# First pass of a two-layer attention kernel: pair tiles between the image tiles, or all behind them

## What is computed

```python
# layer 0: pair_rep is the group-normed x
x = (pair_rep - mu) * rsqrt(var + EPS) * ln_w + ln_b
bias = einsum('hc,bcij->bhij', wb, x)            # 4 heads, added to the scores
scores = einsum('bhcij,bhcik->bhijk', q, k) * scale + bias[:, :, None, :, :]
...
# layer 1
bias = einsum('nijz,zh->nhij', pair_repr, bias_proj)[:, None]   # 8 heads
sim = softmax(einsum('nsqhc,nskhc->nshqk', q, k) * scale) + bias
```

## Time and profile before

| | |
|---|---|
| median of 3 runs | 4822.93 us (4820.17 to 4829.05) |
| the profiled execution | 4825.53 us, its span 4823.7 us |
| mean granted TensorE clock over the span | 0.975 |
| busy over the span | PE 95%, PE weight load 81%, DVE 81%, ACT 78%, POOL 75% |
| DMA | 383.12 MB, mean 79 GB/s over the span |
| first four of 40 slices (0 to 482 us) | 355, 351, 346, 198 GB/s |

### The profile page before, as it was taken

How to read it: one execution, slowest core, us unless ns; L and a number is a source line. 1 busy time by engine, 2 the same in 40 slices (tenths; PEclk the granted TensorE clock), 3 DMA queues, 4 the chain that set the end, 5 groups by cost and what they waited for, 6 DMA issues and landing times. The chain is left out here.

```text
span 4823.7 us, 153371 instructions
## 1 busy us (share of the span) xinstructions
PE 4606.1 (95%) x46135; PEld 3896.8 (81%) x46135; DVE 3924.8 (81%) x12976; ACT 3768.1 (78%) x11664; POOL 3626.7 (75%) x6054
## 2 busy tenths in 40 slices
PE   5667999999999999999999989999999999999998
PEld 1225888888888888888888868888888888888887
DVE  4444888889888988898888968888888888888887
ACT  2336888888888888888888868888888888888886
POOL 3443888888888888888888847777777777777776
PEclk8678999999999999999999989999999999999999
DMA  9996111111111111111111111111111111111111
GB/s 355 351 346 198 58 53 61 52 61 52 61 52 61 53 57 56 53 60 52 61 52 61 53 45 48 52 52 52 52 52 52 52 52 52 52 52 52 52 52 34
DMA packets 237387, 383.12 MB, mean 79 GB/s; under 512 B 18756, under 2 KB 156616, under 8 KB 224968
## 3 DMA queue, kind: packets, MB, share of 16 engines
q1 hardware_dynamic: 237256, 381.63, 23.3%
HBM read 309.21 MB, written 72.35 MB: 79 GB/s over the span
## 5 line engine op out<-in xcount | busy, mean ns | idle before, releaser
L1507 POOL TENSOR_SCALAR l_probs<-l_probs,l_inv 128x256 f32<-128x256 f32 x2048 | 941.5, 479 | 377.5 <-DVE l_inv L1404 377.5
L663 POOL TENSOR_SCALAR l_probs<-l_probs,l_inv 128x256 f32<-128x256 f32 x2048 | 947.8, 477 | 268.5 <-DVE l_inv L914 268.5
L832 ACT ACTIVATE l_probs<-l_probs,l_neg_max 128x256 f32<-128x256 f32 x2048 | 1021.0, 518 | 0.8 <-DVE l_neg_max L906 0.6
L1305 ACT ACTIVATE l_probs<-bank,l_neg_max 128x256 f32<-128x256 f32 x2048 | 942.5, 476 | 46.4 <-DVE l_neg_max L1398 39.4
L906 DVE CUSTOM_DVE_ANT_0 l_probs<-bank,bias 128x256 f32<-128x256 f32 x2048 | 779.9, 418 | 201.1 <-PE bank L773 197.1
L1411 DVE TENSOR_TENSOR l_probs_t<-bank,bias 128x512 f32<-128x512 f32 x1024 | 669.7, 685 | 131.0 <-PE bank L1217 116.0
L1398 DVE TENSOR_REDUCE l_neg_max<-bank 128x2 f32<-128x512 f32 x1024 | 675.0, 682 | 43.1 <-PE bank L1205 33.9
L773 PE MATMUL bank<-ident,l_probs 128*128 128x128 f32 x4096 | 629.5, 276 | 1.1 <-POOL l_probs L663 0.7
L1217 PE MATMUL bank<-ident,l_probs 128*128 128x128 f32 x4096 | 560.0, 274 | 5.3 <-POOL l_probs L1507 3.9
L786 PE MATMUL bank<-l_probs_t,l_v 128*64 128x256 f32 x4096 | 498.5, 385 | 0.2 <-issue 0.2
L773 PEld LDWEIGHTS bank<-ident,l_probs 128*128 128x128 f32 x4096 | 463.9, 141 | 36.8 <-POOL l_probs L663 1.7
(11 more groups left out here) (205 smaller groups left out, 14710.2 us busy)
## 6 DMA issues: line engine op xcount, KB each, us to landing
fp_x<-in_x_dram SPq DMA_DIRECT2D x32, 1024.0 KB, 6.4
fp_ln_w<-in_L_conv_ln_w_dram SPq DMA_DIRECT2D x32, 1024.0 KB, 8.5
fp_ln_b<-in_L_conv_ln_b_dram SPq DMA_DIRECT2D x32, 1024.0 KB, 11.1
fp_pair<-in_L_conv_pair_repr_dram SPq DMA_DIRECT2D x32, 1024.0 KB, 10.6
l_x<-in_x_dram SPq DMA_DIRECT2D x128, 256.0 KB, 2.9
l_ln_w<-in_L_conv_ln_w_dram SPq DMA_DIRECT2D x128, 256.0 KB, 3.3
l_ln_b<-in_L_conv_ln_b_dram SPq DMA_DIRECT2D x128, 256.0 KB, 3.5
x<-l_y SPq DMA_DIRECT2D x128, 256.0 KB, 2.0
```

What stands on the lines that cost most here:

```text
L663: last = nc.gpsimd.tensor_scalar(probs[:, h, c], probs[:, h, c], inv[:, h, c:c + 1], 1.0, ALU.mult, ALU.mult)
L832: last = nc.scalar.activation(probs[:, h, c], probs[:, h, c], ACT.Exp, bias=neg_max[:, h, c:c + 1], scale=-1.0, accum_out=total[:, h, c:c ...
L1305: last = nc.scalar.activation(probs[:, h, c], b_s[h % 4][:, c * W:(c + 1) * W], ACT.Exp, bias=neg_max[:, h, c:c + 1], accum_out=total[:, h ...
L1507: last = nc.gpsimd.tensor_scalar(probs[:, h, c], probs[:, h, c], inv[:, h, c:c + 1], 1.0, ALU.mult, ALU.mult)
```

## The change

All 32 image tiles are run first, and all 32 pair tiles behind them. `over_tiles` is left with image tiles only, in rounds of four with the first peeled. `late_pairs` becomes all tiles. SP loads the first four pair buffers in the last round, once image tile 31 has been issued, and no longer at the start. The statistics and the reload of the parts keep their places relative to the first pair tiles (third to sixth, and second). No operation, size or buffer differs.

```diff
-        def over_tiles(engine, image_tile, image_end, pair_tile):
-            def body(t, first, last):
-                for k in range(2 * PAIR_BUFS):
-                    image = 2 * PAIR_BUFS * t + k, PAIR_BUFS * t + k // 2, k % 2
-                    image_tile(*image)
-                    if last and k == 2 * PAIR_BUFS - 1:
-                        pair_tile(PAIR_BUFS * t + k // 2, t, k // 2)
-                        image_end(*image)
-                    else:
-                        image_end(*image)
-                        if k % 2:
-                            pair_tile(PAIR_BUFS * t + k // 2, t, k // 2)
-            loop_ends_peeled(engine, TILES // (2 * PAIR_BUFS), body)
-        late_pairs = range(TILES // 2, TILES)
+        def over_tiles(engine, image_tile):
+            def body(t):
+                for k in range(4):
+                    image_tile(4 * t + k, 2 * t + k // 2, k % 2)
+            loop_first_peeled(engine, TILES // 4, body)
+        late_pairs = range(TILES)
...
-            for i in range(PAIR_BUFS):
-                load_pair(i, i)
             def body(t, first, last):
-                for k in range(2 * PAIR_BUFS):
-                    if not (last and k >= 2 * PAIR_BUFS - 2):
-                        load_image(2 * PAIR_BUFS * t + k + 2, k % 2)
-                    if last and k == 2 * PAIR_BUFS - 1:
-                        load_pair(PAIR_BUFS * (t + 1) + k // 2, k // 2)
-                        store_pair(PAIR_BUFS * t + k // 2, k // 2)
-                        store_image(2 * PAIR_BUFS * t + k, k % 2)
-                    else:
-                        store_image(2 * PAIR_BUFS * t + k, k % 2)
-                        if k % 2:
-                            load_pair(PAIR_BUFS * (t + 1) + k // 2, k // 2)
-                            store_pair(PAIR_BUFS * t + k // 2, k // 2)
-            loop_ends_peeled(sp, TILES // (2 * PAIR_BUFS), body)
+                for k in range(4):
+                    if not (last and k >= 2):
+                        load_image(4 * t + k + 2, k % 2)
+                    elif k == 2:
+                        for i in range(PAIR_BUFS):
+                            load_pair(i, i)
+                    store_image(4 * t + k, k % 2)
+            loop_ends_peeled(sp, TILES // 4, body)
```

More of the change, by code:

```diff
@@ L423, in image_tile @@
                 project(b_part[B_PART], m.wb_t[:], bt[i]).then_inc(projected[B_PART], 1)
-            def image_end(tile, t, i):
                 pe.wait_ge(weighted, tile + 1)
@@ L441, in pair_project @@
                 project(b_pair, m.w_pair[:], turned[i % 2]).then_inc(pair_projected, 1)
[L443 to L447, removed]
+            over_tiles(pe, image_tile)
             pair_turns(late_pairs[0], late_pairs[0] // PAIR_BUFS, 0)
@@ L481, in pair_out @@
                 nc.scalar.activation(pair_evac[i][:], b_pair[:], ACT.Copy).then_inc(pair_evacuated, 1)
[L483 to L487, removed]
+            over_tiles(act, image_tile)
             pair_copies(late_pairs[0], late_pairs[0] // PAIR_BUFS, 0)
@@ L531, in image_tile @@
                 nc.gpsimd.tensor_tensor(wt[i][:], xt[i][:], wt[i][:], ALU.mult).then_inc(weighted, 1)
-            over_tiles(pool, image_tile, lambda tile, t, i: None, lambda tile, t, i: None)
+            over_tiles(pool, image_tile)
 def finish_statistics(nc, m, pieces):
```

## The result

The changed kernel takes **4838.29 us** (median of 9 runs, 4835.99 to 4839.75), the kernel before on the same chip 4824.85 us (9 runs): ratio 1.0028 [1.0017, 1.0038], slower by 13.4 us. The forecast was 4834.3 us (4822 to 4850), +11.4 us over the kernel before. The profiled execution took 4838.70 us, its span is 4836.9 us.

A forecast was written before the change was run, and what follows sets the result against it. The prediction took the serial PE, POOL, ACT order to bound the mixed image stretch and DMA the pair tiles alone. Terms -40.8 + 51.0 + 1.2 = +11.4 us on 4822.93 gave 4834.3 us, range 4822 to 4850.

The forecast's parts named there:

- Image stretch, step 9.45: Image tiles without pair tiles between them: 9.45 us a tile, 31 steps in 293.0 us against 333.75, a gain of 40.8.
- The buffer loop: Reuse of the two image buffers, from projection through reload to landing: 18.9 us for two tiles, 9.45 a tile.
- the ring: Serial chain in an image tile: PE projects, POOL multiplies, PE projects the product, ACT copies it out; 9.33 us a tile.
- D: Image tile loads, from the first load's issue to the landing of all three parts: forecast 10.04 us.
- C: Image tile, from the start of the weights' projection to the next load's issue into that buffer: forecast 8.76 us.
- The wait between landing and projection: Image tile, PE's wake after its loads have landed: forecast within 0.1 us.
- Rival 1, step 9.33: Image stretch: step at the ring's 9.33 us, cold start hidden, no measurable difference; +6.5 us, 4829.4; chance 0.19.
- Rival 2, faster by the clock: Image stretch: PE's clock rises and stays up, step 8.6 us; -16.2 us, 4806.7; chance 0.07.
- Rival 3, landings of 11.3 us: Image stretch: loads stay slow without pair tiles, step 10.1 us; +30.9 us, 4853.8; chance 0.12.
- The pair stage, +51.0: Pair tiles alone, DMA bound: sixteen more tiles at 3.19 us each add 51.0 us.
- the seam, +1.2: Passage from image to pair tiles: PE arrives cold, so first transposes take longer; +1.2 us, between 0 and 3.4.
- The moves that "cost nothing": Statistics chain, bias reload and DVE bias operations behind pair tiles, and SP's moved pair loads at 0.4 us an issue: 0.

The follow-up runs named there:

- early loads: Changed kernel, but each part of an image tile is loaded as soon as its own buffer is free: 4826.3 us, 1.0002 of the kernel before.
- second banks: Changed kernel, but even and odd image tiles project into PSUM banks of their own: 4840.9 us, 1.0033 of the kernel before.
- filler: Changed kernel plus 24 unused transposes per image tile keeping PE busy: 4838.1 us; with each part loaded once its buffer is free, 4817.9; also with separate banks, 4818.8.
- the four kernels whose loops had been opened: Changed kernel with early loads plus second banks (4814.5 us), plus filler (4817.9), plus both (4818.8), or plus both and stores issued by ScalarE (4815.5).

## Why the prediction was right, and where it was not

*Image stretch, step 9.45.* Measured 9.50, -39.3 us for -40.8. The buffer loop is the bound, as forecast, though narrowly: eight of the 31 steps are the ring's 9.34. Two terms are off and offset each other. D is 10.30 in the mean for 10.04, because the earlier trace rows give one good load, while eight of 30 took 10.6 us or more: +0.13 on the step. C is 8.52 for 8.76, because some product projections were warm: -0.12. The wait between landing and projection is 0.24 for 0.1. The prediction had left the warm projections out against the late loads, so the balance was foreseen, with no number for the loads. That the loop binds is shown by early loads (12 us) against second banks (none).

*Rival 1, step 9.33.* Wrong by the same small margin; with the other loop shortened the step did fall to 9.14.

*Rival 2, faster by the clock.* The clock stayed low (0.62), so its condition did not come about. The filler runs show that its price was wrong as well: it took D to be fixed. With the clock at 0.87 the step was 9.43 and not 8.6, because D grew by what C lost (0.99 and 0.94 us). The Trainium skill (TensorE: Matmul & The Clock Gate, "What's actually happening") has activity release the throttle; the trace agrees: 0.59 without and 0.87 with the filler, from 100 to 280 us.

*Rival 3, landings of 11.3 us.* Three of the first loads came to 11.2 or 11.3, the rest to 11.0 or less; the median is 10.06. Without pair tiles in the queue ln_b landed 9.1 us after its own issue in the median, against 11.1 in the earlier trace rows.

*The pair stage, +51.0, and the seam, +1.2.* Together 52.2 forecast, 51.4 measured. The tiles of the stage are 3.21 us apart for 3.19. Counted from the first pair load behind the reload (344.19, 382.29 before) the stage took 51.5 us more, so the seam's +1.2 is not there at the end: PE lost 0.9 us on the first 32 transposes, the next loads went out 1.1 us later, and by 344.19 us that had been absorbed. The moves that "cost nothing" leave no trace in this sum; PE's idle time behind the reload is 8.90 us (355.19), and 9.05 before. One of their sizes was wrong: SP took 11.32 us for the four pair loads in one go, not 4 x 0.4 (1.81 us with rows of 8 KB). The store of image tile 30 went out at 324.72, over 4 us after its last copy, and nothing waited for it.

*The start.* 1.3 us later, where the prediction had 0. The change is not needed to explain it: runs whose code there is the same began between 26.25 and 28.42 us.

*The layers.* -0.2 us; the prediction had none.

*The absolute time* is 4.0 us above the forecast: 2.0 from the sum, and 1.9 because the kernel before took 4824.85 us beside it and not 4822.93.

*The rate of HBM.* The prediction set aside the Trainium skill's 358 GB/s of the HBM side (DMA: Bandwidth & Descriptors, "Where 436 GB/s comes from") for the 2.5 us per MB of the earlier trace rows. For the changed kernel that was right: its D is made of such loads, and 341 GB/s is what the loop asks for. But the four kernels whose loops had been opened all stop at 8.74 to 8.90 us a step and 357 to 369 GB/s, near the 8.8 us that 3 MB take by the page's figure, an estimate. A single load and a steady row of them have different prices. Whether HBM, or the mixture of loads with stores, sets this rate stays open; only that the stores share a queue is excluded. One reading that was not tried: by the Trainium skill (DMA: Bandwidth & Descriptors, "Why a DMA increments its semaphore by 16 and not by 1") a transfer whose slowest dimension is 4, as in the stores of 4 partitions here, goes to 4 of the 16 DMA engines, whatever queue issues it. Those four would then be last with every load. The traces don't name single engines, but their packets fit. With the stores in ScalarE's queue (q10), 28 to 290 us:

```profile
DMA packets 14652, 96.15 MB, mean 367 GB/s; under 512 B 1875, under 2 KB 1875, under 8 KB 3267
...
q10 hardware_dynamic: 1856, 2.85, 2.9%
```

Of q10's 1856 packets 3267 - 1875 = 1392 carry 2 KB, 12 for each of 116 stores; the other 464 are small ones, 4 for each store. A load has 128 packets of 8 KB and 16 small ones. In the median a packet of 8 KB takes 0.309 us and one of 2 KB 0.084. If 4 engines carry all stores, each of them has 24 x 0.309 + 12 x 0.084 = 8.4 us of work a tile and each of the others 7.4, an estimate, against the measured 8.74 to 8.90. It can't be the whole account, because the mean packet of 8 KB takes 0.349 us and the 16 engines are 0.97 busy in the mean.

## What to carry to other kernels

Where work is taken out of a loop, look for the loop that stood just behind it: here the reuse of two buffers was 0.12 us a tile longer than the ring by the forecast, 0.17 as measured, and the gain ended there. Two loops of one length must be opened together, and a faster engine inside a loop with a transfer buys little if its loads then only queue up behind each other. Work bound by its transfers costs all of them where it stands alone (51.4 us for 16 pair tiles) and less beside a loop that leaves the DMA engines idle (39.3 us for 15 or 16), which is why the mixed order was the better one until both loops were open; the mixed order with both opened was not tried.

## What was not expected of the hardware

- The DMA share is about 1 (0.99) even where PE is busy 55.00 of 55.00 us and every load has landed before it is needed.
- Four 1 MB loads in one go took SP 11.32 us to issue with rows of 1 KB, and 1.81 us with rows of 8 KB.
- A 1 MB load lands 2.5 us behind another in a short row, but a steady row with small stores runs at 357 to 369 GB/s with the DMA engines 0.96 busy, from either queue.
- Four stores of 24 KB take 6.9 us in an empty queue of their own while another queue has loads under way: the queue is not what they wait for.
- With the filler a wait of 2.11 us for a landing was followed by projections of 1.93 us, one of 0.81 us by such of 1.06; without it 0.81 us came before 1.93 as well.
- The first multiplication of identical beginnings lies anywhere from 26.25 to 28.42 us, so a difference of 1 to 2 us at the start says nothing.
